# Log attention on Trainium2: the layer norm's rows normalised by GpSimd with mean and inverse deviation, in place of ScalarE with a bias made by VectorE

## The reference

```python
x = x + attn_a(layernorm(x), W_qkv, W_out)
x = x + ffn(layernorm(x), ...)                 # one shared expert, top 2 of 8 routed ones
x = x + attn_b(layernorm(x), w_qkv, w_ky, w_proj)
x = x + ffn(layernorm(x), ...)

def layernorm(x, eps=1e-05):
    m = mean(x, -1); v = var(x, -1)
    return (x - m) / sqrt(v + eps)

def attn_b(x, w_qkv, w_ky, w_proj):            # 16 heads of 8, eps = 1e-6
    q, k, v = split(x @ w_qkv.T); k_y = x @ w_ky.T
    L = q k^T / sqrt(8); L_y = q k_y^T / sqrt(8)
    agg = sum(exp(clip(L_y, -15, 15)) * mask, -1) + eps
    r = log(abs(L) + eps) - log(agg + eps)
    w = softplus(r) * mask
    return ((w / (sum(w, -1) + eps)) @ v) @ w_proj.T
```

## Time and profile before

| | |
|---|---|
| time, median of 3 runs | 1031.16 us (1024.8 to 1035.87) |
| the profiled execution | 1028.98 us, of which the span of instructions is 1027.1 us |
| busy share of the span | PE 80%, DVE 72%, ACT 55%, POOL 57% |
| log attention, steady steps (450 to 650 us) | DVE 93%, ACT 92%, PE 85%, POOL 53% busy |
| end (800 to 1027 us) | POOL 75%, PE 77% |

### The profile page before, as it was taken

One profiled execution on the slowest core, in us unless ns is written; L12 is line 12 of the kernel. 1 busy time (PEld: TensorE's weight loads), 2 busy tenths in 40 slices (PEclk: granted clock), 3 DMA queues, 4 the chain that ended last, 5 costly groups with the idle time before them and its releaser, 6 DMA issues. The chain is left out here.

```text
span 1027.1 us, 19542 instructions
## 1 busy us (share of the span) xinstructions
PE 819.4 (80%) x6459; PEld 545.3 (53%) x6459; DVE 735.8 (72%) x1506; ACT 568.5 (55%) x805; POOL 586.9 (57%) x815
## 2 busy tenths in 40 slices
PE   3887577899986787888888888979796588899890
PEld 2666566799984333333333333333342256799890
DVE  3888745455563658899999998989789646555574
ACT  1454152133334667989898989998763242233230
POOL 2343486881383666666644444455326877788884
PEclk9999588999997878999999999999877688999996
DMA  9990012123338477584737474732210021132444
GB/s 273 300 131 1 16 39 70 54 81 114 101 84 242 124 197 220 150 227 118 234 108 215 116 208 121 224 106 55 70 42 24 32 75 39 40 102 84 132 135 122
DMA packets 114401, 124.00 MB, mean 121 GB/s; under 512 B 13328, under 2 KB 76560, under 8 KB 114176
## 3 DMA queue, kind: packets, MB, share of 16 engines
q1 hardware_dynamic: 96512, 100.80, 36.2%
q0 software_dynamic: 8416, 17.29, 5.4%
q10 hardware_dynamic: 9376, 4.65, 1.6%
HBM read 59.97 MB, written 62.72 MB: 119 GB/s over the span
## 5 line engine op out<-in xcount | busy, mean ns | idle before, releaser
L2070 DVE TENSOR_SCALAR ring_b<-psum 128x1024 int32<-128x1024 int32 x160 | 194.2, 1216 | 24.0 <-PE psum L1765 20.8
L1930 ACT ACTIVATE ring_a<-psum 128x1024 f32<-128x1024 f32 x160 | 162.4, 1021 | 51.0 <-PE psum L1765 45.7
L1936 ACT ACTIVATE ring_b<-ring_b 128x1024 f32<-128x1024 f32 x160 | 168.7, 1055 | 36.5 <-DVE ring_b L2070 36.1
L2198 POOL TENSOR_SCALAR_AFFINE_SELECT ring_b<-ring_b 128x512 f32<-128x512 f32 (+1 forms) x112 | 80.1, 728 | 171.6 <-ACT ring_b L1936 170.9
L1765 PE MATMUL psum<-stacks 32*128 32x128 f32 (+3 forms) x1024 | 98.9, 385 | 66.2 <-DVE ring_b L2070 36.8
L1765 PEld LDWEIGHTS psum<-stacks 32*128 32x128 f32 x1024 | 56.9, 193 | 173.5 <-ACT ring_a L1930 76.6
L2062 DVE TENSOR_SCALAR ring_a<-ring_a 128x1024 f32<-128x1024 f32 x160 | 119.4, 751 | 16.8 <-ACT ring_a L1930 15.0
L949 ACT ACTIVATE ring_b<-psum 128x512 f32<-128x512 f32 x72 | 42.6, 591 | 114.0 <-PE psum L834 88.0
L1818 PE MATMUL psum<-ring_b,values 128*32 128x256 f32 (+3 forms) x1024 | 94.2, 478 | 8.6 <-POOL ring_b L2198 8.6
L1797 PE MATMUL psum<-ring_a,ones_s 128*32 128x256 f32 (+3 forms) x1024 | 92.3, 469 | 9.8 <-POOL ring_a L2198 9.8
L1092 POOL DMA_INDIRECT r_rows<-y_sorted,rows_of x64 | 67.1, 1048 | 51.3 <-DMA y_sorted<-y_out 39.2
(11 more groups left out here) (220 smaller groups left out, 1484.1 us busy)
## 6 DMA issues: line engine op xcount, KB each, us to landing
stack_q<-parts SPq DMA_DIRECT2D x32, 256.0 KB
stack_ky<-parts SPq DMA_DIRECT2D x32, 256.0 KB
stacks<-stack_q SPq DMA_DIRECT2D x64, 128.0 KB
stacks<-stack_ky SPq DMA_DIRECT2D x64, 128.0 KB
stack_k<-parts SPq DMA_DIRECT2D x32, 256.0 KB
stacks<-stack_k SPq DMA_DIRECT2D x64, 128.0 KB
stack_qr<-parts SPq DMA_DIRECT2D x32, 256.0 KB
stacks<-stack_qr SPq DMA_DIRECT2D x64, 128.0 KB
```

Source lines behind the costliest of these rows:

```text
L1930: nc.scalar.activation(exps[:, n % RING, 2 * u:2 * u + 2, :], psum[:, first:first + 2, :], ACT.Exp, scale=SCALE).then_inc(self.exp, 1)
L1936: nc.scalar.activation(part, part, ACT.Ln, bias=1.0).then_inc(self.ln, 1)
L2070: nc.vector.tensor_scalar(ring[:, m % RING, HEADS_B[u][0]:HEADS_B[u][1] + 1, :].bitcast(I32), psum[:, first:first + 2, :].bitcast(I32), 0x ...
L2198: ins = nc.gpsimd.affine_select(out=part, in_=part, pattern=[[0, part.ap[1][1]], [1, 128]], compare_op=ALU.is_ge, fill=0.0, base=0, channe ...
```

## The change

The four ACT instructions and the DVE instruction for each batch go. POOL takes over: directly behind the last mask of step i = 9 it makes all four tiles of x_hat, as (x - mean) x rstd, with mean and rstd read as one value for each partition. In the lead-in the new steps -11 and -1 of POOL stand behind the powers, among the row fetches. The steps of ACT and DVE stay otherwise as they were, and PE's list is the same but for its line numbers.

```diff
                     self.following.pool_step(p, -12)
+                    self.following.pool_step(p, -11)
                     self.fetch(p, 2, TT, 2 * TT)
                     self.fetch(p, 3, 0, TT)
                     self.following.pool_step(p, -2)
+                    self.following.pool_step(p, -1)
                     self.fetch(p, 3, TT, 2 * TT)
...
-            def normalise(self, a, b, first):
-                a.wait_ge(self.bias_ready, b + 1)
-                if b > 0:
-                    self.wait_made(a, "turn", b - 1)
-                for t in (first, first + 1):
-                    nc.scalar.activation(x_hat[:, t, :], xs(b + 1, t), ACT.Identity, bias=nbias[:, t:t + 1],
-                                         scale=rstd[:, t:t + 1]).then_inc(self.hat, 1)
...
-                if i == 2 and 0 <= a + 1 < B:
-                    self.normalise(a_, a + 1, 2)
...
-                if i == 9 and 0 <= a + 2 < B:
-                    self.normalise(a_, a + 2, 0)
...
-            def vector_bias(self, v, b):
-                v.wait_ge(self.rstd_ready, b + 1)
-                nc.vector.scalar_tensor_tensor(nbias[:], mean_var[:, :, 0], -1.0, rstd[:], ALU.mult, ALU.mult
-                                               ).then_inc(self.bias_ready, 1)
...
-                if i == 8 and 0 <= a + 2 < B:
-                    self.vector_bias(v, a + 2)
...
+            def normalise(self, p, b):
+                p.wait_ge(self.rstd_ready, b + 1)
+                if b > 0:
+                    self.wait_made(p, "turn", b - 1)
+                for t in range(TT):
+                    nc.gpsimd.tensor_scalar(x_hat[:, t, :], xs(b + 1, t), mean_var[:, t, 0:1], rstd[:, t:t + 1],
+                                            ALU.subtract, ALU.mult).then_inc(self.hat, 1)
...
+                if i == 9 and 0 <= a + 2 < B:
+                    self.normalise(p, a + 2)
```

## The result

The change makes the kernel slower. Its median is 1038.75 us (1029.97 to 1045.87, 20 runs) against 1029.15 us of the kernel before (1023.19 to 1037.75, 20 runs); the ratio is 1.0078 with a 95% interval of [1.0055, 1.0101], some 8 us.

What follows compares the result with a forecast made beforehand. It took one loop over ACT, DVE and PE, with ACT and DVE close to full, as the bound. The terms -3.3 - 2.7 + 1.6 + 0.4 = -4.0 us gave 1025.0 or 1027.2, stated as 1026 us, range 1017 to 1037.

Steps and rivals of the forecast that it cites:

- Step 2: At five places ACT's exponential starts 0.77 us sooner, cut to DVE's wait for ACT's split: -3.3 us in all.
- t = 0.35 us: Assumed time of each new POOL normalising instruction, between bounds of 0.25 and 1.24 us; four make 1.4 us.
- the cover: In steady steps POOL's idle time (1.34 us with a fetch) hides the four instructions; later masks cost nothing at first.
- rival 3: POOL's instruction is slow (t = 1.24) and blocks DVE's clips: +9.1 us, 1038.1 us; decides from t = 0.55; chance 0.12.
- steps 9 and 0: Around batch starts, ACT's exponential starts 0.54 us sooner, so POOL's masks and product can too: -2.7 us over four places.
- The lead-in: Before the log attention, POOL's four new instructions delay batch 2's last fetches and the first scores: +1.6 us.
- The four at step -1: POOL's new lead-in instructions ahead of batch 3's last fetches, which are used some 15 us after: no cost.
- The first batch's +0.4 us: In the first batch PE waits for a POOL mask, the next mask comes later too: 0 to 0.8 us, taken as 0.4.
- DVE's bias counted at nothing: DVE's eight dropped instructions mostly wait for a POOL mask: no gain counted, 4.1 us at most for six in steady steps.
- The signs of being wrong: POOL's instruction over 0.55 us, clips over 1 us frequent, or ACT's waits for PE growing by what ACT was spared.
- the likeliest case: The forecast itself for the whole kernel: -4.0 us, stated as 1026 us, its own range 1022 to 1030; chance 0.48.

Runs made afterwards that it cites:

- relief: The kernel before without ACT's 24 normalising instructions of batches 2 to 7, POOL getting nothing and DVE's bias kept; 1025.37 us, ratio 0.9934 to the kernel before.

## Why the prediction was wrong

In short: the step that failed is the one that put POOL's four instructions at 4 x 0.35 = 1.4 us and called them covered in the steady steps, since PE needs the masks of step 0 only "one to two steps (some 5 us each) after". They take 3.98 us there, the room was 2.14 us, and PE's sum waits 1.95 us for the mask. The parts follow.

**Right: what ACT gives.** Step 2: -3.3 us was predicted at five places. Step 2 went from 5.00 to 4.45, 4.99 to 4.35 and 4.99 to 4.22 to 4.23 (three times) in batches 2 to 6, 3.5 us. Not seen was that step 3 gives 1.0 us of it back (4.92 to 5.08 us before, 4.99 to 5.21 after), which leaves 2.5. Steps 9: a gain of 0.54 us per place was read from rows 4, and step 9 is 0.55 to 0.57 us shorter in batches 2 to 5. `relief` measured all together as 6.8 us [3.8, 9.8] for a forecast of 6.0.

**Wrong: t = 0.35 us.** It is 0.79 us, and 1.0 in the steady steps. The bounds of 0.25 and 1.24 held, but the value was taken near the copy and the subtraction, "one tensor is read here and two operations are made on it". A better row was in the trace: DVE runs this very statement in the first block's layer norm.

```profile
L203 DVE TENSOR_SCALAR x_hat<-x_res,mean_var,rstd 128x128 f32<-128x128 f32 x32 | 11.4, 419 | 2.4 <-POOL rstd L197 2.4
```

That row gives 0.42 us on DVE as the least one should expect of POOL, and four times 0.42 is 1.7 us already. The Trainium skill, "GPSIMD Engine Reference", section "Engine selection", says that GpSimd is about twice as slow as VectorE with two inputs and roughly at line rate with one. This instruction has one tensor input, and POOL's 0.79 us against DVE's 0.42 is about the factor that the page gives to two (by medians, 0.79 against 0.34, it is 2.3).

**Wrong, and the step that turned the sign: the cover.** "With that cover gone, the masks of step 0 come later, and PE sums and weights them one to two steps (some 5 us each) after, so that costs nothing at first." The sum does come one step later by number, but the engines are not at the same step at the same time: POOL's masks of step 0 ran from 515.10 to 516.90 and PE's step 1 began its sum at 517.70. The room was 0.8 us, not 5, plus the 1.34 us of idle time. With t = 0.35 the error would have stayed hidden (1.4 us is less than 2.14), so the two mistakes needed each other: the turning point is (1.34 + 0.8) / 4 = 0.53 us per instruction where there is a fetch, close to the 0.55 that rival 3 had from other terms.

**Wrong: steps 9 and 0 as a gain of 2.7 us.** Step 9 gained, but steps 0 and 1 gave it back: 0.08 us in step 0 and 1.17 us in step 1 of batch 4. The prediction looked at one clip only, and there it was right: "if the product starts only behind the clip, the clip is free", and the first clip of step 0 fell from 1.12, 1.80 and 1.80 us to 0.69, 0.74 and 0.74 in batches 2 to 4. Left out was that the delayed masks and product would meet the next clip: it went from 0.68 us to 2.35, 2.53 and 2.52 (1.27 and 1.76 in batches 5 and 6).

**The lead-in, right mechanism, wrong size.** 1.6 us predicted with 4 x 0.35 + 0.2; with the true t the same term is 3.4, and 3.8 was read from power to first scores. "The four at step -1 ... nothing" stands as far as the trace tells. The first batch's +0.4 us can't be judged: its length varies by more (34.4 to 36.2 us over the kernels here).

**DVE's bias counted at nothing** was not tried alone. DVE's busy time rose by 4.1 us in the steady window although the bias went. Held instructions count as busy, and the clips from 400 to 640 us alone are 6.5 us longer in sum.

**The signs of being wrong.** All three that were named came: POOL's instruction takes over 0.55 us, clips of over 1 us went from 6 to 11 between 400 and 640 us, and ACT's waits for scores grew by 10.3 us, more than the 4.4 us that ACT was spared.

**The rivals.** The third, POOL slow and in DVE's way, came nearest with 1038.1 us against 1038.75, but partly by luck. It took t = 1.24 and charged the new instructions themselves with holding two clips. The changed kernel's clips beside the four at 519.23, and the four at step -1 of the lead-in, which no clip disturbs:

```profile
519.08 0.70 DVE L2047 TENSOR_SCALAR ring_a<-ring_a 128x1024 f32<-128x1024 f32 x1
...
520.83 0.68 DVE L2047 TENSOR_SCALAR ring_a<-ring_a 128x1024 f32<-128x1024 f32 x1
...
322.59 3.12 POOL L2190 TENSOR_SCALAR x_hat<-x_res,mean_var,rstd 128x128 f32<-128x128 f32 x4
```

The clips took their usual 0.7 us; it is POOL that was stretched, 3.98 us for four where 3.12 is possible. What held DVE was POOL's old block, shifted. The Trainium skill's rule in "SBUF — State Buffer", "Who interferes with whom", that the one who issues first gets the shared pair for the whole instruction and the other fully blocks, agrees in kind with 1.80, 2.52 and 3.13 us of otherwise 0.8 us or less. Taken for one instruction at a time it would limit the hold to a mask or a product, at most 1.3 us; the runs show it lasting over several POOL instructions in a row, masks and product. The row of four new ones, in contrast, let a clip through in 0.68 us. Why the two rows differ is not shown.

The chances: 0.08 was given to slower by over 1%, 0.79 to within 1%; the ratio lies within 1% at its best estimate and its upper bound touches 1.0101. The error is in the likeliest case, which had 0.48 on a gain of 4 us.

## What to carry to other kernels

An engine's idle time is a cover only up to the moment when somebody needs its next result. Read the room from the timeline, end of the mask to start of the instruction that uses it, not from step numbers, and add only then the idle time ahead of it. Before moving work to POOL look for the same instruction on DVE in the trace and expect about twice its time. And ask not only what the new instruction collides with, but what the instructions behind it, shifted, will collide with: in the steady steps the loss came from these.

## What the runs showed that was not expected

- A tensor_scalar of 128x128 with two operations and per-partition values takes 0.79 us on POOL, 0.36 us on DVE (1.42 us for four) and 0.39 us on ACT.
- A DVE instruction that met POOL's row of masks and product ended only behind the last of them: an addition of 128x128 took 3.13 us, a two-input product 2.78 (a fetch and masks), a clip 2.52. In the row of four tensor_scalars it was POOL that gave way: they took 3.12 us by themselves and 3.1 to 4.8 us in the steps of the log attention, while DVE's clips took their 0.7 us.
- Half the extra load on POOL lengthened step 1 of batches 3 and 4 more than all of it (8.80 against 8.05 and 8.02 us), since it moved the block onto another instruction of DVE. Over the whole kernel it cost less, 7.1 against 11.2 us.
- Odd long steps in otherwise equal places were stretches of lower granted clock: step 3 of batch 7 takes 5.21 us at 1.00, 6.70 at 0.74 and 7.58 at 0.60. The clock of a step should be looked at before its length is explained.
